# Branch hints on three edge-stage loops of a graph-attention and mixture-of-experts kernel

## The reference

```
h = layernorm(x) @ W + b_w
e = leaky_relu(s_dst[dst] + s_src[src] + b_a, 0.2)   # s_* = h @ a[...]
w = exp(e)
alpha = w / segment_sum(w, dst)[dst]
x = x + segment_sum(alpha[:, None] * h[src], dst)
x = x + sum over the 2 chosen of 8 experts of p_e * (gelu(layernorm(x) @ W1[e] + b1[e]) @ W2[e] + b2[e])
```

## Time and profile before

| what | value |
|---|---|
| median of three runs | 864.41 us (862.34 to 867.2) |
| span of the profiled execution, first to last instruction | 861.7 us |
| time of the profiled execution beside its span | not listed with the runs |
| edge stage, first gather to last edge matmul | about 92 to 571 us |
| instructions | 14833 |
| PE busy over the span | 696.6 us (81%) |
| DVE busy | 457.2 us (53%) |
| POOL busy | 457.3 us (53%) |
| ACT busy | 415.4 us (48%) |
| mean granted TensorE clock | 0.921 of full speed |

### The profile page before, as it was taken

The page is one execution under the profiler, slowest core; times in us unless marked ns, Lnnn a source line. Parts: engine busy times, 40 slices in busy tenths (PEclk is TensorE's granted clock), DMA queues, the critical chain, the costliest instruction groups (busy, mean ns, idle before and its releaser), DMA issues.

```text
span 861.7 us, 14833 instructions
## 1 busy us (share of the span) xinstructions
PE 696.6 (81%) x3260; PEld 553.6 (64%) x3261; DVE 457.2 (53%) x1232; ACT 415.4 (48%) x1134; POOL 457.3 (53%) x530
## 2 busy tenths in 40 slices
PE   4999355879888787879788888959889999999960
PEld 3777245657766666667676767845547787888840
DVE  5998223555555555556465555668485433333320
ACT  4443442545545554536455545618754444545430
POOL 5000575666666666666666666310105677777750
PEclk9999687998989899989999898988988999999995
DMA  5342576666666666666656666407993577777768
GB/s 197 117 155 92 156 213 164 172 188 168 186 181 174 178 177 182 186 171 183 189 166 184 176 179 179 118 27 283 334 380 127 104 131 131 135 131 135 130 91 250
DMA packets 58299, 146.96 MB, mean 171 GB/s; under 512 B 8868, under 2 KB 18708, under 8 KB 57880
## 3 DMA queue, kind: packets, MB, share of 16 engines
q0 software_dynamic: 35216, 106.84, 50.6%
q1 hardware_dynamic: 22968, 37.16, 12.3%
q10 hardware_dynamic: 80, 2.56, 1.0%
HBM read 118.17 MB, written 33.47 MB: 176 GB/s over the span
## 4 chain that ended last, share of the span: by engine, by line
PE 40%; issue 19%; DVE 11%; DMA 11%; ACT 4%; POOL 4%; POOLq 2%; DVEq 2%; another core or an unknown queue 2%; ACTq 1%; SPq 1%
PE ps L705 30%; DMA result<-y,si 8%; PE ps L659 3%; POOL rows L506 2%; DMA x_all<-in_x_dram 2%; ACT E L951 2%; ACT ps L951 2%; PE ps L844 1%; DVE Wt L1217 1%; PE ps L785 1%; DVE S L1228 1%; DVE acc L1235 1%; PE ps L755 1%; POOL xg L593 1%
## 5 line engine op out<-in xcount | busy, mean ns | idle before, releaser
L705 PE MATMUL ps<-rows,S 128*128 128x257 f32 x1556 | 383.4, 404 | 98.7 <-issue 83.9
L506 POOL DMA_INDIRECT rows<-node_table,srcT x313 | 301.8, 964 | 234.4 <-issue 83.8
L705 PEld LDWEIGHTS ps<-rows,S 128*128 128x128 f32 x1556 | 312.3, 202 | 169.6 <-issue 121.3
L951 ACT ACTIVATE E<-sdst_b,rows 128x128 f32 x389 | 124.0, 389 | 236.2 <-DVE Wt L1217 120.7
L1235 DVE TENSOR_TENSOR acc<-acc,ps 128x514 f32 x99 | 68.0, 687 | 116.1 <-remote 77.6
L1228 DVE SCALAR_TENSOR_TENSOR S<-ps,lane,Wt 128x128 f32<-128x128 f32 x389 | 109.6, 345 | 4.4 <-issue 0.8
L951 ACT ACTIVATE ps<-sdst_b,rows 128x128 f32 x313 | 96.2, 351 | 2.0 <-issue 2.0
L844 PE MATMUL ps<-W_e,xgT 128*128 x352 | 83.4, 380 | 0.0
L602 POOL DMA_INDIRECT result<-y,si x44 | 70.4, 1601 | 11.4 <-issue 7.1
L1222 DVE TENSOR_TENSOR lane<-dstT,node_id 128x4 f32 (+1 forms) x98 | 16.1, 164 | 111.5 <-issue 77.0
L844 PEld LDWEIGHTS ps<-W_e,xgT 128*128 128x128 f32 x352 | 63.4, 190 | 6.9
(11 more groups left out here) (203 smaller groups left out, 678.8 us busy)
## 6 DMA issues: line engine op xcount, KB each, us to landing
W_e<-in_L_ffn_W_dram SPq DMA_DIRECT2D x16, 512.0 KB, 8.5
node_table<-rows SPq DMA_DIRECT2D x20, 258.0 KB, 2.7
result<-acc SPq DMA_DIRECT2D x20, 256.0 KB, 2.5
xn_table<-xn SPq DMA_DIRECT2D x20, 256.0 KB, 2.2
rows<-node_table,srcT POOLq DMA_INDIRECT x313
x_all<-in_x_dram SPq DMA_DIRECT2D x19, 256.0 KB, 3.1
out_dram<-result SPq DMA_DIRECT2D x1, 2500.0 KB, 16.7
out_dram<-result ACTq DMA_DIRECT2D x1, 2500.0 KB, 18.4
```

The costliest lines, as they stand in the source:

```text
L506: nc.gpsimd.indirect_dma_start(out=rows[:, g % RING, c, :], out_offset=None, in_=table, in_offset=bass.IndirectOffsetOnAxis(ap=srcT[:, GC ...
L705: m = pe.matmul(ps_agg[q][:, a, 0:HALF], S[:, w, c, :], rows[:, r, c, a * HALF:(a + 1) * HALF], start=(c == 0), stop=(c == n - 1))
L951: m = nc.scalar.activation(e[:, c, :], sdst_b[:, bass.ds(tile * P, P)], ACT.Exp, bias=bias, scale=scale)
```

## The change

Nothing else is added, removed or moved, and no wait or semaphore changes. In the inner loops over further tiles no hint is put. In all the hint is executed 8 times on PE, 9 times on ACT and 18 times on DVE.

```diff
-            with pe.Fori(1, NG // RING) as i:
+            with nc.Fori(1, NG // RING, engines=[pe.engine], hint_back_edge=True) as i:
                 window_words(pe, regs, i)
                 for r in range(RING):
                     group(RING * i + r, r, i)
...
-            with act.Fori(0, NG // RING) as i:
+            with nc.Fori(0, NG // RING, engines=[act.engine], hint_back_edge=True) as i:
                 window_words(act, regs, i)
                 for r in range(RING):
                     group(r, i)
...
-            with dve.Fori(1, NG // U) as i:
+            with nc.Fori(1, NG // U, engines=[dve.engine], hint_back_edge=True) as i:
                 window_words(dve, regs, i, BACK, U)
                 for r in range(U):
                     step_of_group(U * i + r, r, i)
```

## The result

| | before | changed |
|---|---|---|
| median | 862.59 us (19 runs, 859.96 to 869.88) | 868.07 us (19 runs, 862.64 to 871.19) |
| span of the profiled execution | 861.7 us | 866.2 us |
| mean granted TensorE clock | 0.921 | 0.917 |

The ratio is 1.0055, with a 95% interval from 1.0039 to 1.0071. The change costs about half a per cent: 4.7 us by the ratio, 5.5 us by the medians, 4.5 us by the two spans. The forecast was +1.2 us. The kernel before now stands at 862.59 us; the 864.41 us to which the forecast was added were the median of its first three runs.

A forecast was written before the change was run, and what follows sets the result against it. It took PE's matmuls, about 39 of each 47.2 us, plus queue holes as the bound. Heads +1.1 us (PE 0.6, DVE 0.5, ACT 0) and loop end +0.1 gave +1.2 on 864.41: 865.6 us, range 858 to 873.

The forecast's parts named there:

- the likeliest case: Whole kernel: +1.2 us, to 865.6 us, with a range of its own from 862.4 to 871.4 us.
- At the end of a loop: Loop exits: the last hint is wrong, so code behind may come later; bound +0.6 us, taken as +0.1 us.
- The sum at the heads: Loop heads: added hints cost 0.12 us at five PE heads, 0.10 at five DVE heads, ACT 0; +1.1 us.
- no fetch on each pass: Edge loops: nothing is reloaded on a pass, so there seems no fetch for a hint to bring forward.
- ACT's hints at nothing: ACT's loop heads: hints hidden behind queued activations, cost 0; without that cover 0.9 us.
- The give-back: Branches back on PE and DVE: the hint might remove turning-round time, up to 2.0 us; taken as 0.
- The rule of the Trainium skill: Loop branches: a taken branch with its target in neither 16 KiB line waits for a fetch, making the hint worthwhile.
- The first, late instructions filled by the hint: Holes after DVE heads: the hint fills them, more than 4.3 us faster, perhaps about 843 us; chance 0.08.
- The second, a dear hint: Ten heads on the path: a hint costs like a load of words, 13.8 us, or 878 us; chance 0.20.
- The third, nothing at all: All heads: target there and hint covered by queued work, 864.4 us; chance 0.71 together with the forecast.

The follow-up runs named there:

- more loops: The changed kernel with the hint also on five further loops of PE, ACT and DVE in the routing and expert stages: 868.72 us, ratio 1.0067 to the kernel before.

## Why the prediction came near in time and missed the mechanism

The forecast was no change (+1.2 us, chance 0.71). The result, +0.55% (0.39 to 0.71), can't be told from the line of 0.5% to slower: 868.07 is inside the range from 858 to 873 and inside the likeliest case's own range, but the mechanism is neither that case's nor a rival's. So that the number lies in the range is luck in good part. Of the +1.2 us, 1.1 stood for something that costs nothing. The sum was also put on 864.41 us, 1.8 above the 862.59 of all runs; this took 1.8 us off a distance of 4.3.

**The step that failed is "At the end of a loop"**: "If code behind the loop came later for it, I bound this by the longest hole of the same kind, 1.82, so +0.6 us; I take +0.1." It named the right place and the right cause. But the late code left a hole of 3.28 us, which counts whole, against a bound of 0.6, and with the slower matmuls behind it the term came to about +4.5 us. Two things were missing:

- *The bound was taken from the wrong kind of hole.* The 1.82 us and the 1.20 us are mostly the load of window words. A hole at a head whose code is there says nothing about one whose code has to be fetched. The row that would have said more was open to me: the q8 packets. I counted them from 200 to 540 us to see whether passes fetch anew, and began the stretch just behind the packet at 196.93 us, which is the block for the exit. The right question was not how many packets there are in the loop, but which of them is made ahead and what the engine needs for that. The Trainium skill, in "Runtime: NRT & Kernel Launch", section Instruction fetch mechanics, says that the sequencer fetches the next page while it executes the current one, in sequence. The packet at 196.93 us before, in the middle of the first pass, agrees; the one at 549.32 us after doesn't, since it comes 0.9 us after PE's matmuls have run out. That an open hint puts it off is in no row before.
- *What a hole can cost behind itself.* The granted clock went from 1.00 to 0.63 for 4 us behind a hole of 3.28 us (to 0.50 with the hint on PE alone). With 12 matmuls instead of 20 in those 4 us, 8 x 0.2 = 1.6 us of work are put off; by the chain the net loss is 1.2 us. The hole of 1.20 us before let it stand at 1.00.

That it is PE's block, and the hint in every pass, is shown: PE alone gives the whole loss (1.0057), ACT and DVE alone nothing (0.9996, 0.9997), and it is gone, with the packet back near 197 us, when the hint doesn't say "taken" in the first pass (1.0000), when it says so only in the last (1.0002), and when it stands behind the body (0.9998). The profiles put the loss at one place. From the start of the last gather to the end of the last edge matmul it is 26.0 to 28.4 us in the four kernels with a hint "taken" in every pass on PE (the change, its repeat, PE alone, more loops), and 22.7 to 24.0 us in the other nine with all gathers. That the hint stops the fetch *because* the queue then follows the named branch only is argued from these, not shown.

**The sum at the heads, +1.1 us, was nothing.** Its prices were fair: I took 0.12 us on PE and 0.10 on DVE for a hint with its gap, and the rows of 31 and 44 ns with 0.03 us of issue give 0.06 and 0.07; I had left out that inner tests get dearer by 68 ns, 79 times on DVE. But five heads on PE and five on DVE were put on the path because the chain that ended last runs through them, and there nothing is worth its length: 18 DVE hints and 79 dearer tests cost nothing (0.9997), 35 other instructions cost nothing (0.9995), and taking PE's 1.9 us loads away from all its heads, in exchange for a small one a group, gains nothing (1.0004). The period follows the gathers (36.2 us with three of four), and the queues' time disappears in it. The hole at the head near 499 us, which was to grow from 1.82 to 1.9, is 0.73 us in the changed kernel, and the two behind the DVE head near 232, 1.01 and 6.18, became 1.23 and 5.20: these holes come out otherwise in each profile.

**Right:** no fetch on each pass (2 packets on q14 and none on q8 from 200 to 540 us, as before), so nothing for a hint to bring forward; the hint's row between 0.03 and 0.10 us, 14868 instructions, 14 and 21 packets, a period of 47.2 us on the mean (single passes now take 45.7 to 49.8 us, by PE's branch back), loads at 1.936 and 0.819 us; and ACT's hints at nothing. The give-back of up to 2.0 us was rightly taken as 0: the branch on PE went up by 0.02 us, not down by 0.14. The rule of the Trainium skill that the prediction weighed, a fetch for each taken branch out of two lines, was rightly not followed.

**The rivals.** The first, late instructions filled by the hint, is out: PE's "issue" in the edge stage is 79.0 us in 63 places (83.9 in 71), the holes behind DVE heads are there, and the time rose. The second, a dear hint, is out by its row (31 to 44 ns) and by the kernels with one engine's hints. Its sign was right, and its 0.20 was the nearest thing to the outcome, for another reason. The third, nothing at all, holds in time for 27 of the 35 hints, those of ACT and DVE.

**Open:** why the hint holds the fetch back; why the time from the late packet to PE's next matmul differs (2.4 and 4.8 us); whether the kernel without "taken" in the last pass loses 0.1%; and whether the changed kernel's early q14 packets, two of which are missing near 150 us, matter where PE isn't late. No kernel here that computes the same sums beats the one before.

## What to carry to other kernels

In these loops no instruction packet comes with a pass, so a hint on the back edge had nothing to bring forward; with "taken" in every pass, it put off the block that follows the loop. Whether a hint pays in a loop whose passes do fetch, no run here shows. Look at when instruction packets move, not at how many there are. If a hint is wanted, let it say "not taken" in one pass (the first, 1.0000) or put it at the bottom (0.9998). Don't price a hole by its length on the chain that ended last: change its cause once and see (here moving 1.9 us of loads away from each head was worth nothing), and look for places with nothing behind them, such as the exit of a loop near the last transfer.

## What the runs showed of the hardware

- An open hint "taken" makes other compare-and-branches dearer: 56 to 124 ns on DVE (L1265), 45 to 99 on ACT (L959), 208 to 217 on PE (L716). With the hint at the bottom they stay at 56, 45 and 208.
- PE's instruction packets are 16 KB (q8, 14 packets, 0.23 MB), those of the other engines' queue 8 KB (q14, 21 packets, 0.17 MB).
- A hint "taken" in every pass of PE's loop put off the packet of the block behind the loop from 197 us to the exit; "not taken" in the first or in seven passes didn't.
- After a hole of 3.28 us the granted TensorE clock was 0.63 over the next 4 us, and 1.00 after that, while a hole of 1.20 us left it at 1.00. In the kernel with the hint only in the last pass, holes of 1.08 and 1.04 us with one matmul between them were followed by 0.50 from 540 to 544 us; there it cost nothing, since gathers were still to come.
- A load of one word into a PE register takes 302 ns, of eight words 1.944 us.
- Without a quarter of the gathers PE's "issue" idle time falls from 18% to 7% of the stretch, with PE's queue instructions unchanged.
